# Cross-attention and mixture-of-experts layer: the loops over the attention batches written out on five engines

## The reference

```python
x = x + xattn(layernorm(x), ctx, ctx)     # q, k, v, softmax(q k^T / 4) v, We, biases
h = layernorm(x)
probs = softmax(h @ router_w + router_b); top_w, top_idx = top_k(probs, 2)
for e in range(8):
    x = x + comb[:, e:e+1] * (gelu(h @ expert_up[e].T) @ expert_down[e].T)
```

## Time and profile before

| | us |
|---|---|
| median of 3 runs | 425.81 |
| lowest and highest | 423.88, 426.14 |
| profiled execution, time | 423.66 |
| profiled execution, span | 421.9 |
| TensorE busy | 388.4 |
| VectorE busy | 240.7 |
| ScalarE busy | 195.9 |
| GpSimd busy | 165.5 |

### The profile page before, as it was taken

One profiled execution on the slowest core, in us unless ns is written; L12 is line 12 of the kernel. 1 busy time (PEld: TensorE's weight loads), 2 busy tenths in 40 slices (PEclk: granted clock), 3 DMA queues, 4 the chain that ended last, 5 costly groups with the idle time before them and its releaser, 6 DMA issues.

```text
span 421.9 us, 9337 instructions
## 1 busy us (share of the span) xinstructions
PE 388.4 (92%) x2235; PEld 315.3 (75%) x2236; DVE 240.7 (57%) x690; ACT 195.9 (46%) x357; POOL 165.5 (39%) x253
## 2 busy tenths in 40 slices
PE   8989889989998889898999999999999999999960
PEld 6756665766666569896888888888888888888850
DVE  4674957899799767762337646373723633332320
ACT  3455434434434346334447747474744744444420
POOL 2333022120302121145555656645564464546441
PEclk9999999999999999999999999999999999999995
DMA  8902010410211111542326655564742223222221
GB/s 273 358 34 99 2 50 2 151 50 2 86 64 50 52 53 50 167 125 51 53 36 166 200 149 136 139 160 117 186 99 38 38 38 51 34 42 38 38 38 12
DMA packets 26387, 37.19 MB, mean 88 GB/s; under 512 B 4705, under 2 KB 17441, under 8 KB 26369
## 3 DMA queue, kind: packets, MB, share of 16 engines
q1 hardware_dynamic: 19312, 26.98, 19.2%
q0 software_dynamic: 7056, 9.99, 14.7%
HBM read 27.18 MB, written 9.79 MB: 88 GB/s over the span
## 4 chain that ended last, share of the span: by engine, by line
PE 70%; issue 10%; DVE 6%; SPq 4%; ACT 3%; POOL 3%; DMA 2%; POOLq 0%; DVEq 0%; ACTq 0%
PE bankC L1573 14%; PE bankC L1219 9%; PE bankC L1221 9%; PE bankC L1220 9%; PE bankC L1574 7%; PE bankB L1551 6%; PE bankA L1543 2%; PE bankA L1313 2%; PE bankC L1301 1%; DVE put L955 1%; DMA raw<-down 1%; PE bankB L1314 1%; PE bankB L1219 1%; POOL qk_l L379 1%; SPq L316 1%
## 5 line engine op out<-in xcount | busy, mean ns | idle before, releaser
L1573 PE MATMUL bankC<-dn_w,qk_h 128*128 x256 | 94.4, 407 | 1.2 <-DVE qk_l L1154 1.2
L1574 PE MATMUL bankC<-dn_w,qk_l 128*128 x256 | 71.9, 281 | 0.0
L460 POOL DMA_INDIRECT out<-x2T,idx_s x32 | 51.5, 1610 | 18.8 <-issue 18.8
L1573 PEld LDWEIGHTS bankC<-dn_w,qk_h 128*128 128x128 f32 x256 | 48.2, 188 | 11.7 <-issue 1.4
L1219 PE MATMUL bankC<-up_w,xnT_h 128*128 (+1 forms) x128 | 53.1, 415 | 1.0 <-DVE xnT_l L1148 1.0
L1161 DVE SCALAR_TENSOR_TENSOR x2T<-bankC,gate,x2T 128x256 f32<-128x256 f32 x32 | 15.5, 483 | 61.8 <-ACT x2T L682 48.3
L1221 PE MATMUL bankC<-up_w,xnT_l 128*128 (+1 forms) x128 | 50.7, 396 | 0.0
L1220 PE MATMUL bankC<-up_w,xnT_h 128*128 (+1 forms) x128 | 50.6, 395 | 0.0
L1574 PEld LDWEIGHTS bankC<-dn_w,qk_l 128*128 128x128 f32 x256 | 48.2, 188 | 0.0
L677 ACT ACTIVATE raw<-bankC 128x512 f32<-128x512 f32 x64 | 38.4, 600 | 20.3 <-PE bankC L1221 20.3
L450 POOL DMA_INDIRECT xr<-rows,idx_g x35 | 39.5, 1128 | 20.3 <-issue 20.3
(11 more groups left out here) (258 smaller groups left out, 828.5 us busy)
## 6 DMA issues: line engine op xcount, KB each, us to landing
xall<-up SPq DMA_DIRECT2D x24, 256.0 KB
xall<-down SPq DMA_DIRECT2D x24, 256.0 KB
rows<-xr SPq DMA_DIRECT2D x4, 528.0 KB
raw<-up SPq DMA_DIRECT2D x4, 512.0 KB, 3.9
raw<-down SPq DMA_DIRECT2D x4, 512.0 KB, 4.8
out<-xall SPq DMA_DIRECT2D x4, 512.0 KB, 2.8
xall<-x SPq DMA_DIRECT2D x1, 1536.0 KB, 8.3
cst<-const SPq DMA_DIRECT2D x1, 640.0 KB, 8.4
```

Source lines behind the costliest of these rows:

```text
L460: g.indirect_dma_start(out, bass.IndirectOffsetOnAxis(idx_s[:, n:n + 1], 0), y[n], None, bounds_check=T + P - 1, compute_op=ALU.add).then_ ...
L1573: mm(bankC[:, 2, :], hT_h[:, o], wd, start=(m == 0), stop=False)
L1574: last = mm(bankC[:, 2, 0:D], hT_l[:, o], wd[:, 0:D], start=False, stop=(m == KF - 1))
```

## The change

The `Fori` of the attention batches becomes a Python loop on all five engines. The functions called are the same; i is now a Python number, so each pass is emitted on its own, and all addresses and waits in it are constants. The loops of the expert stage stay as they are.

```diff
@@ sync @@
             load01(0)
-            with sp.Fori(1, B) as i:
+            for i in range(1, B):
                 load01(i)
                 store(i - 1)
@@ gpsimd @@
-            with pool.Fori(1, B) as i:
+            for i in range(1, B):
                 key_blocks(i)
                 halves_rstd2(i - 1)
                 value_blocks(i)
@@ scalar @@
-            with act.Fori(1, B) as i:
+            for i in range(1, B):
                 batch(i)
@@ vector @@
             batch(1, False)
-            with dve.Fori(2, B) as i:
+            for i in range(2, B):
                 batch(i, True)
@@ tensor @@
             batch(1, False)
-            with pe.Fori(2, B) as i:
+            for i in range(2, B):
                 batch(i, True)
```

## The result

| | before | after |
|---|---|---|
| median, runs side by side on one chip | 424.27 (11 runs) | 421.95 (11 runs) |
| lowest and highest | 423.32, 427.11 | 420.14, 423.96 |
| profiled execution, time | 423.66 | 421.42 |
| profiled execution, span | 421.9 | 419.6 |

The ratio is 0.9937, with a 95% interval of 0.9912 to 0.9963: 2.7 us less by the ratio and 2.3 us by the medians, where 1.5 us were forecast and "no measurable change" was given the most weight. The measured 421.95 us lies just under the low end of the predicted range, 422.0. The gain is just past the 0.5% that the prediction took for what a measurement tells from nothing. Runs over 1.5% above the fastest of their kernel are left out of every ratio and every count in this document.

A forecast was written before the change was run, and what follows sets the result against it. TensorE, busy 92% of the span, was taken as the bound, with gains only in the attention batches. Terms 0.57 + 0.72 + 0.05 + 0.24 = 1.58, rounded to 1.5 us off 425.81, gave 424.3 us; range 422.0 to 426.6.

The forecast's parts named there:

- step 1: TensorE's seam between batches 2 and 3, L1373 to L1313: 1.72 us falls to 1.15, 0.57 us less.
- Step 2: First eight matmul pairs of batches 2 and 3 on TensorE, without register arithmetic: 0.32 + 0.40 = 0.72 us less.
- Step 3: Entry of TensorE's loop, first matmul released by VectorE's logits: 0.05 us less, bounds 0 and 0.38.
- Step 4: VectorE's register work between L939 and L945: 0.12 us per loop pass comes through, 0.24 us less.
- Step 5: Exit of the loop: nothing gained, as TensorE still waits 0.56 us for VectorE's msum_bf.
- Rival B: VectorE keeps the pace: TensorE waits for it by as much as it came forward, 425.8 us stands; 17 in 100.
- Step 6: ScalarE, GpSimd and SyncE in all three passes: nothing gained, covered by their waiting for TensorE.
- Step 7: Longer programs: at most two more code transfers of about 0.84 us each; taken as 0, bound 1.7 us.
- Rival A: Registers cost everywhere: batches 2 and 3 shrink to 34.60 us each, 3.0 us in all, 422.8 us; 12 in 100.
- Rival C of the prediction: Code comes too late in the expert loop, making the kernel slower; 5 in 100.

The follow-up runs named there:

- e4: Kernel before, TensorE's two-pass loop made two one-pass loops: counter and never-taken branch stay, constants instead of register arithmetic; no time given, seam 1.00 us.
- e6: Kernel before with one wait fewer (v_hot dropped) at each slot matmul; 425.03 us in a single execution.
- e3: Kernel before with all engines' attention loops written out except TensorE's; 424.72 us, ratio 0.9962.
- e2: Kernel before with only TensorE's attention loop written out; 421.75 us, ratio 0.9894.
- e1: Kernel before run again with no edit, with its profile; 425.15 us, ratio 0.9976.
- e7b: Changed kernel with one wait fewer (v_hot dropped) at each slot matmul; 421.8 us, ratio 0.9897.
- e10b: Changed kernel with no further edit, run beside the filled ones; 422.42 us, ratio 0.9912.
- e11: Kernel before with matmuls of zeros only ahead of the turn of the logits in each batch; 425.23 us, ratio 0.9993.
- e8b: Kernel before with TensorE's idle spots in batches, tail and ahead of the first expert tile filled by matmuls of zeros; 422.43 us, ratio 0.9934.
- e9b: Changed kernel with TensorE's idle spots in batches, tail and ahead of the first expert tile filled by matmuls of zeros; 420.1 us, ratio 0.9862.
- e13: Changed kernel with all the filling by matmuls of zeros and one wait per slot matmul; 419.76 us, ratio 0.9882.

## Why the prediction was wrong

It named the right mechanism and the right places, and priced one of them too low, step 1; a second source of time, the clock, it did not have at all.

- **Step 1, the seam: wrong in size.** Predicted 1.15 us left, measured 0.77, so 0.95 us instead of 0.57. The step "written out, even the exit's 83 + 32 ns are gone: 1.27 - 0.12" is the one that failed. I took the loop's exit as the form without registers and took off the branch alone. But the exit is still inside the loop: its four slot matmuls had an ALU_OP and a wait instruction each. e4 puts these at 0.39 us at the exit, and e6, where one wait and its arithmetic less took 0.42 us off the exit with the loop in place, shows the same from the other side.
- **Step 2, the eight pairs: right.** 0.31 + 0.39 us, predicted 0.32 + 0.40, from the same eight in the tail.
- **Step 3, the entry: right.** 0.66 us from L1373 to L1313, for 0.70.
- **Step 4, VectorE: right on VectorE, short on TensorE.** L939 to L945 lost 0.13 us, for 0.12. But from L1249 to L1373 TensorE gained 0.18 + 0.19 us in the two batches, for the 0.24 predicted. With VectorE's part and the others' alone (e3) it gained 0.11 + 0.16, with TensorE's alone (e2) 0.09 + 0.08. The last is what step 1 left out too: the first half of the slot matmuls, ahead of the logits, also has its arithmetic. e3's attention is 0.51 us shorter in all, so the others' loops may be worth up to twice the 0.24.
- **Step 5, the exit: right in the net.** L1373 to L1388 took 3.77 us and takes 3.76. But the wait for `msum_bf` did not "remain near 0.56 us": TensorE came 0.55 us earlier and waits 0.54 us longer. Rival B is right here and only here.
- **Step 6: right** as far as e3 bounds it. **Step 7: right.** Two more transfers, and no gap of TensorE for them. Where the written-out code passes them, the segments are 9.78 us as before. The 0.84 us for a transfer is known only roughly: after's row, 10 transfers and 0.2%, gives 0.002 x 16 x 419.6 / 10 = 1.34 us by the same sum.
- **The sum.** As measured, 0.95 + 0.70 + 0.04 + 0.37 = 2.06 us for steps 1 to 4, against 2.05 in the attention and 1.98 between the filled kernels. Predicted were 1.58, written down as 1.5. Of the 0.48 between, 0.38 is step 1.
- **What was missing: the clock.** All my rows had a granted clock of 1.00, and none was from 139 to 204 us. The profiled execution had a half-clock stretch there, worth 1.4 us. Unfilled kernels with TensorE's loop kept were low in 55 of 67 runs of before, 9 of 12 in e1 and 9 of 12 in e3; those with TensorE's taken branch and registers gone in 4 of 11 (after), 0 of 6 (e2), 5 of 9 (e4), 4 of 8 (e7b) and 4 of 9 (e10b). That is 73 of 91 against 17 of 43, and within a session 21 of 24 against 0 of 6 and 5 of 9, and 18 of 20 against 4 of 8 and 4 of 9. That the change makes low runs rarer is therefore shown; why is in part argued. At the seam a reason lies near: the idle spot there, after which e1 and e11 fell to half clock (at 100.5 and 102.0 us), is closed: 0.42 us idle ahead of L1313 before, none after. With the tail filled in both, the kernel with the idle spot was low in 4 of 12 runs (e8b), the ones without it in 0 of 12 (e9b, e13), which speaks for it.
- **Rival A fell:** the gain sits at the seam and in the pairs behind it, and the inner segments of 9.79 and 14.46 us are unchanged. **Rival C of the prediction fell:** no run shows a back edge that waits for a transfer of code, on which the 5 in 100 for it and its part in the 0.08 for "slower" rest. In after the 42 branches on TensorE's sequencer at the expert loop (L1609 and L1611) took 67 to 237 ns each, where a transfer is 0.84 us by the prediction's estimate. From 204 to 400 us TensorE is busy without a gap, as this row of after's busy time by stretch has it.

```profile
204.00:400.00 196.00, 196.00 (x1112) 168.24 (x1111) 92.58 (x194) 106.97 (x200) 106.38 (x177) 1.00 0.42 93
```

Part of the surprise is also the yardstick. The forecast of 424.3 us was taken off 425.81; the result is 3.9 us below that and 2.3 below the eleven runs' 424.27. So 1.5 of the 2.4 us by which the time was missed are the yardstick's. Before scatters with its half-clock stretches (the low runs of e1 have a median 2.45 us above its other three), and three runs of it were too few to say where its median is.

Left open: why the written-out kernel also drops less often in the tail, where its code is the same. It arrives there at another time relative to the DMAs, but no run parts that from chance; e7b, with nearly the same code there, did drop once, at 175.9 us. Open too is how the 0.33 us part between the taken branch and the fused waits, since no loop with registers and without a taken branch could be had.

## What to carry to other kernels

The loop over registers cost TensorE nothing here in the 24 us of a pass where its matmuls are long or wait for data: 9.79 and 14.46 us with registers, 9.78 and 14.46 us with constants. It cost 0.95 us at the seam, and 0.31 and 0.39 us at the eight pairs, which have register arithmetic between them: count such places, at the exit as well. When a trace serves as the witness for the form without registers, see that every instruction in the row is free of them.

Read the granted clock over the whole span and in several runs, not in the stage that the change touches alone. If a few idle spots of TensorE let the clock fall, a few matmuls of zeros in them may be worth as much as the change: here the filling gave 0.7%, the change 0.6 to 0.9%, and both together 1.2 to 1.4%.

## What the runs showed of the hardware

- **A taken branch of TensorE was short beside a transfer of code.** The branch back over 188 matmuls took 237 to 238 ns in each of the seven profiled executions with the loop, where a transfer of code takes 0.8 to 1.3 us by the estimates above, worked out from the queue rows of before and after. One that is not taken took 76 to 83 ns in them and 67 to 81 in e4.
- **Register arithmetic is small, but here it was in series with short matmuls.** The 14 ALU_OP entries of before at the slot matmuls (L1403) took 32 ns each, yet one wait and its arithmetic less at four slot matmuls gave 0.51 us at the seam (e6): 0.13 us for each matmul. With constants, one wait less at the same four gave 0.10 us (e7b).
- **Half clock behind idle spots.** Six profiled executions had half-clock stretches ahead of the last matmul (before, e1, e3, e6, e7b, e11), eleven in all. Each was some 3.4 us at a granted clock of 0.50, and those at the seam of e1 and behind L1388 cost 1.2 to 2.1 us each. In the 2 us ahead of each TensorE was partly idle, busy 0.47 to 1.77 us: 1.23 us of 1.70 ahead of the one at the seam (e1), 0.96 of 2.00 ahead of the one at 177.9 (before). Not every such spot was followed by one: after kept a clock of 1.00 behind 1.17 us busy of 2.00.
